# Attention in a fused macaron block: four slots for the f16 halves, weighing three pieces behind, side products taken out a step later

## The reference

```python
qkv = x @ W_qkv                       # 16 heads of 64
q, k = apply_rope(q), apply_rope(k)   # t * cos + rotate_half(t) * sin
dots = einsum('bhid,bhjd->bhij', q, k) * scale
dots = where(causal, neg, dots)
attn = softmax(dots, axis=-1)
out = einsum('bhij,bhjd->bhid', attn, v)
out = relu(out @ W_o1) @ W_o2         # then a layer norm
```

## Time and profile before

| | |
|---|---|
| median of 3 runs | 5959.87 us (5954.83 to 5964.68) |
| the profiled execution | 5942.21 us |
| its span in the trace | 5940.3 us |
| busy, share of the span | PE 66%, DVE 74%, ACT 40%, POOL 45% |
| attention_heads, batch 0, first qk copy to last add to acc | 3323.5 to 4357.0 us |
| attention_heads, batch 1, the same | 4439.1 to 5468.5 us |

### The profile page before, as it was taken

The page is one execution under the profiler, slowest core; times in us unless marked ns, Lnnn a source line. Parts: engine busy times, 40 slices in busy tenths (PEclk is TensorE's granted clock), DMA queues, the critical chain, the costliest instruction groups (busy, mean ns, idle before and its releaser), DMA issues. The chain is left out here.

```text
span 5940.3 us, 81715 instructions
## 1 busy us (share of the span) xinstructions
PE 3936.9 (66%) x27691; PEld 2390.1 (40%) x27691; DVE 4405.1 (74%) x5229; ACT 2385.7 (40%) x3604; POOL 2650.9 (45%) x1626
## 2 busy tenths in 40 slices
PE   3976555444444545489495388888855888888395
PEld 2652111111111111156385155555633555556384
DVE  6873799999999999988301578888866888887301
ACT  1223432333333333212221166667743666667231
POOL 0211676676676776512202056655303646650202
PEclk9998655566666555599598599999977999999597
DMA  2000000000000000000254222222102212220254
GB/s 73 0 4 6 0 0 0 0 0 0 0 0 0 0 0 0 15 0 0 87 170 127 73 46 54 54 46 46 35 29 55 54 43 51 53 52 6 89 183 136
DMA packets 216325, 235.76 MB, mean 40 GB/s; under 512 B 61547, under 2 KB 181284, under 8 KB 214880
## 3 DMA queue, kind: packets, MB, share of 16 engines
q1 hardware_dynamic: 206304, 207.35, 13.1%
q0 software_dynamic: 8704, 24.35, 1.2%
q10 hardware_dynamic: 1024, 0.13, 0.0%
HBM read 116.95 MB, written 31.59 MB: 25 GB/s over the span
## 5 line engine op out<-in xcount | busy, mean ns | idle before, releaser
L971 PE MATMUL mix_scan_y<-mix_scan_hc,ident 128*128 128x512 f32 x512 | 476.9, 1086 | 957.1 <-DVE mix_scan_hc L904 957.1
L2040 DVE TENSOR_TENSOR att_b_prob_low<-att_b_prob,att_b_prob_high 128x1024 f16<-128x1024 f32 (+2 forms) x640 | 780.8, 1220 | 237.3 <-ACT att_b_prob_high L2002 223.7
L895 DVE TENSOR_TENSOR_SCAN mix_scan_h<-mix_scan_a_bar,mix_scan_state,mix_scan_dub 128x512 f32<-128x512 f32 x256 | 834.1, 3297 | 0.1
L2067 DVE TENSOR_REDUCE att_b_neg_max<-att_b_peek 128x1 f32<-128x1024 f32 (+7 forms) x768 | 684.3, 905 | 75.5 <-PE att_b_peek L1897 39.1
L2008 ACT ACTIVATE att_b_prob<-att_b_score,att_soft 128x1024 f32<-128x1024 f32 (+2 forms) x640 | 631.9, 987 | 169.6 <-PE att_b_score L1917 102.7
L852 ACT ACTIVATE mix_scan_a_bar<-mix_val,mix_A 128x512 f32 (+1 forms) x256 | 170.8, 714 | 1219.4 <-DVE mix_scan_h L895 1219.4
L971 PEld LDWEIGHTS mix_scan_y<-mix_scan_hc,ident 128*128 128x128 f32 x512 | 149.9, 323 | 1233.8 <-DVE mix_scan_hc L904 1102.0
L2002 ACT CAST att_b_prob_high<-att_b_prob 128x1024 f16<-128x1024 f32 (+2 forms) x640 | 587.9, 919 | 30.4 <-PE att_b_o L1945 13.1
L1941 PE MATMUL att_b_o<-att_b_vh,att_b_prob_high 128*128 128x65 f16 x4352 | 465.4, 195 | 179.4 <-DVE att_b_heads L2058 88.6
L1941 PEld LDWEIGHTS att_b_o<-att_b_vh,att_b_prob_high 128*128 128x128 f16 x4352 | 400.6, 98 | 306.3 <-DVE att_b_prob_low L2040 205.9
L816 POOL TENSOR_TENSOR mix_scan_dub<-mix_u,mix_scan_b_row 128x512 f32<-128x512 f32 x128 | 279.7, 2185 | 412.8 <-ACT mix_scan_b_row L856 412.8
(11 more groups left out here) (329 smaller groups left out, 9595.6 us busy)
## 6 DMA issues: line engine op xcount, KB each, us to landing
moe_w<-in_L_ffn_W_dram SPq DMA_DIRECT2D x64, 1024.0 KB, 8.1
att_b_crossed<-att_b_raw SPq DMA_DIRECT2D x512, 64.0 KB, 2.0
att_b_q_both<-att_b_halves SPq DMA_DIRECT2D x256, 64.0 KB, 2.0
att_b_k_twice<-att_b_halves SPq DMA_DIRECT2D x256, 64.0 KB, 2.0
moe_slots_in<-moe_route_zero SPq DMA_DIRECT2D x2, 4096.0 KB, 14.2
moe_exp_x<-moe_slots_in SPq DMA_DIRECT2D x32, 256.0 KB, 4.2
moe_slots_out<-moe_exp_y POOLq DMA_DIRECT2D x32, 256.0 KB, 6.5
att_b_k_low<-att_b_halves SPq DMA_DIRECT2D x128, 64.0 KB, 2.0
```

The lines of the kernel that those rows point to most:

```text
L895: dve.tensor_tensor_scan(cols(hs, 0, m), cols(a_bar, b, m), cols(dub, b, m), state[:, at:at + 1], ALU.mult, ALU.add).then_inc(scanned, 1)
L971: done = pe.matmul(y_ps[m][:, :], ident[:, :], cols(hc, n % 2, m), start=(n == 0), stop=(n == S_N - 1))
L2040: dve.tensor_tensor(prob_low[:, at:at + width], prob[:, at:at + width], prob_high[:, at:at + width], ALU.subtract).then_inc(low_ready, 1)
L2067: last = dve.tensor_reduce(neg_max[:, first + col:first + col + 1], peek_ps[:, base:base + nb * P], AX.X, ALU.max, negate=True)
```

## The change

- RING = 4: prob_high and prob_low get four slots; prob and the scores keep two. The halves of piece m wait for the weighing of piece m-4, not m-2.
- BEHIND = 3: PE weighs piece v-3 in step v, and DVE takes a chunk out a step later.
- Side jobs: PE issues them in the same step as before. ACT and DVE take them out in step v+1, on ACT between high_part and exponents, on DVE between low_part and take.
- In the prologue side jobs are taken out in their own step, but also ahead of take and maximum. The eighth qk job moves from step 17 to step 15, and the stack transfers are issued by ACT: stack(i-2) ahead of the copy of job i, the last two behind the last copy.
- wo and headsT get one slot in place of two. SP loads wo behind the fifth stack of a turn (in the last turn at its start), and turn i on ACT waits for all products of the turned heads before.

```diff
+BEHIND = 3
+RING = 4
...
-    if v not in SIDE or not has_pair(kind, SIDE[v][2]):
+    jobs = {15 if kind == BEFORE and u == 17 else u: job for u, job in SIDE.items() if has_pair(kind, job[2])}
+    if v not in jobs:
         return None
...
                 if has_pair(kind, 0):
-                    load_out_weights(t, b)
                     spread_queries(t, b, 1)
+                if kind == LAST:
+                    load_out_weights(t)
                 if has_pair(kind, 1):
                     cross(t, 0)
                     for i in range(QK_JOBS):
                         if i + 1 < QK_JOBS:
                             cross(t, i + 1)
-                        stack(t, b, i, kind)
+                        if kind != BEFORE:
+                            stack(sp, t, b, i, kind)
+                        if i == 4 and has_pair(kind, 0):
+                            load_out_weights(t)
...
-                    if v >= 2 and has_piece(kind, v - 2) or v < 2 and has_piece(kind, -1):
-                        weigh(t, b, v - 2)
+                    if has_piece(kind, v - BEHIND):
+                        weigh(t, b, v - BEHIND)
...
                     if has_piece(kind, v - 1):
                         high_part(t, v - 1)
+                    job = side_job(kind, v if kind == BEFORE else v - 1)
+                    if job:
+                        if kind == BEFORE and job[0][0] == "qk" and job[0][1] >= 2:
+                            stack(act, t, b, job[0][1] - 2, kind)
+                        side(t, b, *job[0])
+                        if kind == BEFORE and job[0] == ("qk", QK_JOBS - 1, 1):
+                            for i in (QK_JOBS - 2, QK_JOBS - 1):
+                                stack(act, t, b, i, kind)
                     if has_piece(kind, v):
                         exponents(t, v)
...
-                    job = side_job(kind, v)
-                    if job:
-                        side(t, b, *job[0])
...
-                    act.wait_ge(o_ready, out_count(p, 2 * (i - 1) if i >= 2 else 0))
-                    act.copy(headsT[:, i % 2 * GRP:(i % 2 + 1) * GRP], side_ps[:, :]).then_inc(hT_ready, 1)
+                    act.wait_ge(o_ready, out_count(p, 2 * i))
+                    act.copy(headsT[:, :], side_ps[:, :]).then_inc(hT_ready, 1)
...
-                wait_unless_first(act, p_done, piece(t, m - 1))
-                act.copy(prob_high[:, at:at + width], prob[:, at:at + width]).then_inc(high_ready, 1)
+                wait_unless_first(act, p_done, piece(t, m + 1 - RING))
+                act.copy(prob_high[:, to:to + width], prob[:, at:at + width]).then_inc(high_ready, 1)
...
                     if has_piece(kind, v - 1):
                         low_part(t, v - 1)
-                    if v >= 2 and has_piece(kind, v - 2) or v < 2 and has_piece(kind, -1):
-                        take(t, b, v - 2)
+                    job = side_job(kind, v if kind == BEFORE else v - 1)
+                    if job:
+                        side(t, b, kind, *job[0])
+                    if has_piece(kind, v - BEHIND):
+                        take(t, b, v - BEHIND)
                     peek_at = slot_at(kind, v)
                     if peek_at:
                         maximum(t, *peek_at)
-                    job = side_job(kind, v)
-                    if job:
-                        side(t, b, kind, *job[0])
```

More of the change, by code:

```diff
@@ L1581, in side_job @@
 def side_job(kind, v):
-    if v not in SIDE or not has_pair(kind, SIDE[v][2]):
+    jobs = {15 if kind == BEFORE and u == 17 else u: job for u, job in SIDE.items() if has_pair(kind, job[2])}
+    if v not in jobs:
         return None
-    earlier = [SIDE[u] for u in sorted(SIDE) if u < v and has_pair(kind, SIDE[u][2])]
+    earlier = [jobs[u] for u in sorted(jobs) if u < v]
     before = {BEFORE: None, FIRST: ("mrow", 0, 0)}.get(kind, ("out", 5, -1))
-    return SIDE[v], ([before] + earlier)[-1]
+    return jobs[v], ([before] + earlier)[-1]
 def in_turns(eng, turn):
@@ L1631, in attention_heads @@
         prob = sb("prob", [P, 2 * SPAN])
-        prob_high, prob_low = sb("prob_high", [P, 2 * SPAN], F16), sb("prob_low", [P, 2 * SPAN], F16)
+        prob_high, prob_low = sb("prob_high", [P, RING * SPAN], F16), sb("prob_low", [P, RING * SPAN], F16)
         neg_max, max_row = sb("neg_max", [P, 2 * (QT + SB)]), sb("max_row", [QT, 2 * P], F16)
         inv = sb("inv", [P, GT])
-        heads, headsT = sb("heads", [P, QT * PAIR]), sb("headsT", [P, 2 * GRP])
+        heads, headsT = sb("heads", [P, QT * PAIR]), sb("headsT", [P, GRP])
         score = [ps("score0", SPAN), ps("score1", SPAN)]
@@ L1686, in rotate, with stack @@
             assert c.n == ROPE_STEPS
+        def stack(eng, t, b, i, kind):
+            r = i % 2
+            at = (1 - b) * SEQ + i // 2 * GRP
+            to = slice(at, at + GRP)
+            ready, through = qk_count(t + 1, i + 1), piece(t, 0)
+            if i == 0 and not isinstance(t, int):
+                ready, through = eng.to_reg(ready), eng.to_reg(through)
+            eng.wait_ge(roped, ready)
+            if i == 0 and kind in (MIDDLE, LATE):
+                eng.wait_ge(scored, through)
+            for h in range(2):
+                mine = slice(h * HEAD, (h + 1) * HEAD)
+                if r == 0:
+                    eng.dma_start(q_both[h][0:HEAD, to], high(r)[mine, :]).then_inc(stacked[r], 16)
+                    eng.dma_start(q_both[h][HEAD:P, to], low16(r)[mine, :]).then_inc(stacked[r], 16)
+                else:
+                    eng.dma_start(k_twice[h][0:HEAD, to], high(r)[mine, :]).then_inc(stacked[r], 16)
+                    eng.dma_start(k_twice[h][HEAD:P, to], high(r)[mine, :]).then_inc(stacked[r], 16)
+                    eng.dma_start(k_low[h][0:HEAD, to], low16(r)[mine, :]).then_inc(stacked[r], 16)
         @block.sync
@@ L1713, in load_weights, with load_out_weights @@
                                  .rearrange("(c p) n -> p c n", p=P)).then_inc(w_loaded, 16)
-            def load_out_weights(t, b):
-                before, used = (sp.to_reg(t * 16), sp.to_reg(out_count(t - 1, 0))) if not isinstance(t, int) else \
-                    (t * 16, out_count(t - 1, 0))
+            def load_out_weights(t):
+                before, used = (sp.to_reg(t * 16), sp.to_reg(out_count(t, 0))) if not isinstance(t, int) else \
+                    (t * 16, out_count(t, 0))
                 wait_unless_first(sp, wo_loaded, before)
                 wait_unless_first(sp, o_ready, used)
-                sp.dma_start(wo[:, b * D:(b + 1) * D], dram["W_o1"][bass.ds(t * PAIR, PAIR), :])\
+                sp.dma_start(wo[:, :], dram["W_o1"][bass.ds(t * PAIR, PAIR), :])\
                     .then_inc(wo_loaded, 16)
@@ L1737, in cross @@
                         .then_inc(crossed_over[i % 2], 16)
[L1739 to L1757, removed]
             in_turns(sp, turn)
@@ L1875, in side @@
                     for j in range(2):
-                        at = i // 2 % 2 * GRP + (i % 2 * 2 + j) * P
+                        at = (i % 2 * 2 + j) * P
                         last = pe.matmul(side_ps[:, j * D:(j + 1) * D], headsT[:, at:at + P],
-                                         wo[:, mine * D:(mine + 1) * D], start=True, stop=True)
+                                         wo[:, :], start=True, stop=True)
                     last.then_inc(o_ready, 1)
@@ L2038, in low_part @@
                 dve.wait_ge(high_ready, piece(t, m + 1))
-                wait_unless_first(dve, p_done, piece(t, m - 1))
-                dve.tensor_tensor(prob_low[:, at:at + width], prob[:, at:at + width], prob_high[:, at:at + width],
+                wait_unless_first(dve, p_done, piece(t, m + 1 - RING))
+                dve.tensor_tensor(prob_low[:, to:to + width], prob[:, at:at + width], prob_high[:, to:to + width],
                                   ALU.subtract).then_inc(low_ready, 1)
```

9 lines of the change are left out of this document (4 added, 5 removed).

## The result

The changed kernel took 5993.81 us (median of 4 runs, 5991.17 to 6000.3) against 5960.65 us for the kernel before on the same chip: 1.0058 times as long, 95% interval 1.0041 to 1.0075. It is slower, by 33 us, and lies outside the range that was given.

The account below looks back on a forecast made before the run. POOL's serial rope chain was taken to bound A, DVE's work B. -63 + 7 - 2 + 22 = -36 us from the profiled 5942.2 gives 5906; with the median 17.7 above, 5924 us, range 5852 to 5980.

Parts of the forecast that it names:

- B: Stretch from a turn's eighth qk copy to the next turn's first, 62.7 us: -4.5 us each, -63 for fourteen.
- weighing three behind: In the turns, PE no longer weighs a piece whose low half was made the step before; priced at nothing.
- The work that was to move out of B: low(17) and maximum(18), 1.89 + 0.81 us at the start of B, move into A, where POOL hides them.
- A: Stretch, turn's first to eighth qk copy, POOL's chain: one more low half falls in, +0.5 us each, +7 for fourteen.
- The lower bound: Least gain per B, -1.8 us: only moved work less new idle, if v copies make PE's step the longer.
- The wait at B's start: DVE idle for 2.5 us at the start of B, where it stood 1.60 before.
- Rival 1: Side products on DVE stand ahead of maxima that PE's next peeks wait for: +67 us in the turns, 5991; 17%.
- The last pair: Its first steps, without qk jobs, run at DVE's pace: -1 us a block, -2 us in all.
- The prologue: Before turn 0: vl ahead of maximum on DVE lengthens v steps, 2.92 to 4.6 us, PE clock near half; +11 a block, +22.
- the head start: Prologue's eighth copy at 39.6 us against 45.8, by a shorter slot round; only -0.5 us left at maximum(18).
- wo and headsT: Single slots and the moved load of wo in the turns: new waits met by step 6, cost nothing.
- The slots: Rings of four for the halves: slot wait 0.3 us in B, waits in A beside POOL's chain worth nothing.

Follow-up runs that it names:

- run 7: run 2 with weighing and taking two pieces behind in place of three: 0.9983 of the kernel before.
- run 1: Kernel before with only the side products of the turns taken out a step later on ACT and DVE: 0.9994 of the kernel before.
- run 12: run 7 with all five GpSimd rope operations of the turns over 64 of 512 columns, the rest left out: 0.9672, median 5759.09 us.
- run 13: run 2 with all five GpSimd rope operations of the turns over 64 of 512 columns, the rest left out: 0.9693, median 5772.03 us.
- run 2: Changed kernel with the maximum ahead of DVE's part of a side product in the prologue: 1.0030 of the kernel before.
- run 3: run 2 with the side products of the turns back in their own step too: 1.0035 of the kernel before.
- run 10: run 7 with the side products of the last pair and of what follows it in their own step: 0.9963 of the kernel before.
- run 15: Kernel before with run 10's prologue and single wo and headsT; side products in their own step, two slots, weighing two behind: 0.9997.
- run 11: Kernel before with GpSimd's first multiply of each rope of the turns over 64 of 512 columns, the rest left out: 0.9929.
- run 4: Kernel before with single wo and headsT alone, wo's load moved behind the turn's fifth stack: 0.9998 of the kernel before.
- run 6: run 5 with weighing and taking two pieces behind in place of three: 1.0001 of the kernel before.
- run 14: run 10 with two slots in place of four for the halves: 0.9972 of the kernel before.
- run 5: run 4 with the rings of four, weighing and taking three pieces behind: 1.0033 of the kernel before.

## Why the prediction was wrong

The step that failed is the term of B, -4.5 us each, -63 in all, and with it the price of nothing for weighing three behind. A B came out 0.6 us longer (63.5 to 64.1, mean of twelve).

- **The work that was to move out of B.** I took low(17) and maximum(18), 2.7 us, out of B at its start and did not ask what comes in at its end. B ends with the next turn's first copy, which also goes a step later, so a low half of the other end falls into B: 23.0 low halves a B and 17.0 an A in the traces of before and of run 7 alike. In number nothing moved. The lower bound that I had set, -1.8, is what the edit gives by itself (-1.8 and -1.7 in runs 1 and 7), and that it fits is luck, as it has another source: DVE's busy time falls by 1.5 us a B (run 7), most of it in shorter low halves (mean 1.149 to 1.097 us, 23 of them, 1.2 us). Of that, 0.8 is the exchange at the two ends: the low half that leaves took 1.89 us, beside GpSimd's ropes, the one that comes in, the next turn's first, takes 1.09. DVE's waits, which were to shrink, do not (6.2 us before, 6.5 in run 7), as peeks take the place of the high half and vh. The wait at B's start, forecast at 2.5 us, was 1.48.
- **Weighing three behind** was counted as a wait removed. It is a wait exchanged (table under run 7), and the step costs 0.33 to 0.47%, 20 to 28 us, the largest single term of the result. About half of the cost goes away with GpSimd's ropes; what the other half is stays open (runs 12 and 13). I had named what decides a piece's pace, "one peek bank" among it, and not asked what PE waits for there once it does not wait for the low half.
- **Rival 1** had the outcome right and the place wrong. PE does wait for maxima, but the side products in front of them are not why; they cost nothing two behind (run 1) and nothing three behind (run 2 against run 3). Its price, 5991 us, is met by luck.
- **The last pair** was -2 us. Its first steps are the same 36.8 us as before; steps 16 to 39, which I had not looked at, take 55.1 us against 47.3, 7.7 a block, and runs 1 and 10 show that the later place costs 5 to 6 of them; in run 3, without it but weighing three behind, they take 49.3, 2.0 more than before.
- **The prologue** was right in what costs and in how much: v steps take 5.2 to 6.1 us at a granted clock of 0.50 to 0.72, not 2.9 at 1.00, and the new order on DVE costs 10.6 us a block (run 2), where I took 11.5. The whole lost 8.2 a block against 11, since more of the head start survives than the 0.5 that I took: maximum(18) starts 51.4 us behind the first copy, forecast 53.1, before 53.6. On the head start I misread the rows. The eighth copy comes at 39.6 us, as worked out, but "the round is shorter" is wrong: the seventh copy comes 2.9 us later than before, and the 45.8 of before was the eighth copy's wait for PE in step 17, not a slot's round. By these rows the 6 us come of the job's move to step 15, and the stacks on ACT gave none of them; no run takes these two edits apart. The Trainium skill (DMA: Bandwidth & Descriptors, § Issuing engines are not separate DMA queues) gives the issuing of transfers from a second engine little, and no run here shows more (run 15: 0.9997).
- **A** came near in size, +0.7 us (55.9 to 56.6) against +0.5, and GpSimd's chain is the limit (run 11), if a near one. The reason was wrong, so the size is luck: no low half more falls into A (17.0 before and after), and GpSimd is busy for 49.5 us over the six ropes in both traces. Their chain grew from 51.1 to 51.6 us by idle time, and in 3 of 14 As the eighth copy now waits for PE.
- **wo and headsT** at nothing: right (run 4). **The slots** at nothing: right (runs 6 and 14).

The measured parts, by differences of ratios: weighing three behind +0.47%, the prologue's new DVE order +0.28%, and the rest of the change, which is run 7, -0.17%. They add up to the 0.58% by construction, since each is the difference of two neighbours in one row of kernels; in another order the parts can differ, as the 0.33% of runs 5 and 6 does.

## What to carry to other kernels

When two engines hand small pieces to and fro, a wait that is removed from one engine's list comes back at the next thing that it needs from the same partner, unless the partner's own list gets shorter: follow the list on to the next wait before counting a gain. When an edit shifts all events of a loop by a step, cut the stretch at both ends and count the instructions in it before and after; what leaves at one end enters at the other. And look for the places where a new order has no cover: here the prologue and the stretch from the seventh B on lost 13 us of a block's 22, the As and Bs between them 9.

## What the runs showed of the hardware

A low half of 128x1024 (two SBUF inputs, one output) on VectorE takes 1.22 us where GpSimd is idle, and up to 2.4 us in B where GpSimd's ropes run (run 2, turn 4). With the ropes cut to an eighth of their columns the mean low half in A fell from 1.35 to 1.09 us and A from 56.9 to 43.7 us (run 7 to run 12). The Trainium skill (GPSIMD Engine Reference, § Specifications) states such contention, and these runs agree with it. I had not expected its weight: the same 23 low halves of a B take 25.2 us in run 7 and 27.0 in run 2, and the two Bs differ by 1.9.

In A, the granted clock fell with the later side products from 0.97 to 0.92 (means over twelve, before and run 7), and PE's busy time rose from 46.0 to 47.9 us for nearly the same instructions.
